# A hybrid layer on one core: four batches stage by stage, or two groups of two batches with stages interleaved

## What is computed

```
x = x + ssm(ln(x))     # gated selective scan, 16 states per channel
x = x + ffn(ln(x))     # dense + 2 of 8 experts, chosen once per batch
x = x + att(ln(x))     # retention, then attention over its output
x = x + ffn(ln(x))     # the same weights as above
```

## Time and profile before

| | us |
|---|---|
| median of 3 runs | 1385.68 (1381.11 to 1390.2) |
| the profiled execution | 1391.36, span 1389.4 |
| busy of the span: PE, ACT, DVE, POOL | 1071.3, 975.3, 742.7, 325.7 |
| granted PE clock, mean | 0.915 of full speed |

### The profile page before, as it was taken

How to read it: one execution, slowest core, us unless ns; L and a number is a source line. 1 busy time by engine, 2 the same in 40 slices (tenths; PEclk the granted TensorE clock), 3 DMA queues, 4 the chain that set the end, 5 groups by cost and what they waited for, 6 DMA issues and landing times. The chain is left out here.

```text
span 1389.4 us, 17492 instructions
## 1 busy us (share of the span) xinstructions
PE 1071.3 (77%) x5850; PEld 393.9 (28%) x5850; DVE 742.7 (53%) x1012; ACT 975.3 (70%) x884; POOL 325.7 (23%) x194
## 2 busy tenths in 40 slices
PE   4748777777799956777446888888888888679996
PEld 3213333333344422332341111111111111134443
DVE  5869998987566648998481001200300300256664
ACT  3767665754688832221336999999999999658885
POOL 3117776766111114665100000000000000011110
PEclk8769999999899978998777999999999999879998
DMA  2000100100100000000001111111111111000002
GB/s 73 0 16 30 31 30 30 60 30 31 32 30 30 31 24 0 0 0 1 8 0 33 24 24 32 37 24 28 22 33 34 24 24 28 11 31 31 30 30 61
DMA packets 24188, 36.48 MB, mean 26 GB/s; under 512 B 7362, under 2 KB 11970, under 8 KB 24130
## 3 DMA queue, kind: packets, MB, share of 16 engines
q1 hardware_dynamic: 24130, 35.71, 9.5%
HBM read 16.82 MB, written 6.29 MB: 17 GB/s over the span
## 5 line engine op out<-in xcount | busy, mean ns | idle before, releaser
L1674 ACT ACTIVATE att_prob<-att_s_ps 128x1536 f32<-128x1536 f32 x342 | 459.2, 1912 | 7.4 <-PE att_s_ps L1588 7.3
L1603 PE MATMUL att_o_ps<-att_prob,att_va 128*32 128x512 f32 x2048 | 273.9, 607 | 0.5 <-ACT att_prob L1674 0.5
L1705 DVE COPY att_o_sb<-att_o_ps 128x512 f32<-128x512 f32 x32 | 22.1, 691 | 381.7 <-PE att_o_ps L1603 381.7
L1588 PE MATMUL att_s_ps<-att_q_st,att_k_st 32*128 32x512 f16 x1024 | 134.4, 388 | 80.8 <-ACT att_prob L1674 76.1
L685 POOL TENSOR_TENSOR scan_hc<-scan_state,scan_c_rep 128x1024 f32<-128x1024 f32 x64 | 151.9, 2392 | 71.9 <-DVE scan_state L642 71.7
L787 POOL TENSOR_TENSOR ffn_veps<-ffn_mv,all_eps 128x4 f32<-128x4 f32 x16 | 9.1, 570 | 575.3 <-DVE ffn_mv L944 575.3
L642 DVE TENSOR_TENSOR_SCAN scan_state<-scan_decay,scan_drive_ps 128x1024 f32<-128x1024 f32 x64 | 142.9, 2270 | 0.3 <-ACT scan_decay L615 0.3
L282 PE MATMUL scan_y_ps<-scan_hc,all_ident 128*128 128x512 f32 x256 | 130.2, 634 | 8.3 <-DVE scan_y_sb L661 6.2
L1588 PEld LDWEIGHTS att_s_ps<-att_q_st,att_k_st 32*128 32x128 f16 x1024 | 33.1, 91 | 327.2 <-ACT att_prob L1674 315.9
L619 ACT ACTIVATE scan_c_rep<-scan_c_ps 128x1024 f32<-128x1024 f32 x64 | 65.4, 1022 | 80.4 <-PE scan_c_ps L282 80.1
L1012 DVE SCALAR_TENSOR_TENSOR ffn_hid_lo<-ffn_hid,ffn_share,ffn_hid_hi 128x1024 f16<-128x1024 f32 x64 | 81.9, 1283 | 48.8 <-ACT ffn_hid_hi L920 48.1
(11 more groups left out here) (215 smaller groups left out, 1505.8 us busy)
## 6 DMA issues: line engine op xcount, KB each, us to landing
ffn_w_sel<-w_split SPq DMA_DIRECT2D x16, 512.0 KB, 3.2
w_split<-scan_w_parts SPq DMA_DIRECT2D x8, 512.0 KB, 2.9
att_q_st<-hv_part SPq DMA_DIRECT2D x64, 64.0 KB, 2.1
att_k_st<-hv_part SPq DMA_DIRECT2D x64, 64.0 KB, 2.1
ln_x_half<-in_x SPq DMA_DIRECT2D x8, 256.0 KB, 2.8
scan_w_raw<-in_w1e SPq DMA_DIRECT2D x8, 256.0 KB, 3.2
scan_w_raw<-in_w2e SPq DMA_DIRECT2D x8, 256.0 KB, 3.4
out<-store_out SPq DMA_DIRECT2D x8, 256.0 KB, 2.4
```

The costliest lines, as they stand in the source:

```text
L1588: last = pe.matmul(s_ps[e % 2][:, n, :], k_st[rows, g % 2, kc * P:(kc + 1) * P], q_st[rows, g % 2, HALVES[half]], start=True, stop=True)
L1603: last = pe.matmul(o_ps[half][32 * j:32 * j + 32, :], va[:, g % 2, kc, j, :], prob[:, (GH * v + j) % RING, :], start=kc == 0, stop=kc == K ...
L1674: act.activation(prob[:, first % RING:first % RING + n, :], s_ps[e % 2][:, 0:n, :], ACT.Exp).then_inc(exped.sem, 1)
```

## The change

Batches 0 and 1 form the first group, 2 and 3 the second. `hybrid_layer` runs load, layer norms and scan inputs for all four, then the selective scan of the first group alone. `group` then runs `mixture`, `queries_and_keys` and `attention` on the first group, with the second group's scans as `following`. The second group's `mixture` holds four feed-forwards (the first ones of batches 2 and 3, the second ones of 0 and 1) and the retentions of 2 and 3; its attention is plain. A last `mixture` holds the second feed-forwards of 2 and 3.

`mixture` replaces `ffn` and `retention`. It is one block in slots s. A feed-forward batch takes 24 slots, 12 for each half of 512 tokens, with the same operations at half the width; y is made by ACT instead of DVE, and x is turned directly, without ACT's staging copy. A retention starts its norm at slot 25 (batch 0 of the list) or 49, and has 16 units of half width (8 rows, two halves of time), in two slots of three from 8 slots after its norm, or one a slot if no feed-forward lies beside. The decay is made as a tanh, halved and shifted by DVE (`open_gate`). Loops are written out. The nine weight splits lie in 32 scan steps, at 1, 4, 7, ... 25. Constants of retention, queries, attention and the scan's `a_neg` are made in `load_constants`. A stage's semaphores are cleared by POOL at its end.

```diff
+                sp.dma_start(w_all[:, 0:len(RET_MATS), :], d["ret_mats"]).then_inc(ret_loaded, 16)
+                sp.dma_start(w_all[:, len(RET_MATS):W, :], d["wsv"]).then_inc(ret_loaded, 16)
+                sp.dma_start(t.head_sum[:, :, :], d["head_sum"]).then_inc(att_loaded, 16)
+                sp.dma_start(t.qk_mats[:, :, :], d["att_mats"]).then_inc(att_loaded, 16)
+                sp.dma_start(t.qk_rows[:, :, :], d["bqk"]).then_inc(att_loaded, 16)
+                sp.dma_start(t.wo[:, :], d["wo"]).then_inc(att_loaded, 16)
...
+                act.wait_ge(ret_loaded, 16 * 2)
+                act.activation(t.ret_hi[:, :, :], w_all[:, :, :], ACT.Copy, scale=WS).then_inc(ret_high, 1)
...
+                for k in range(E + 1):
+                    sp.wait_ge(w_scaled.sem, w_scaled.before(k, 0, 1))
+                    sp.dma_start(w_raw[:, 0, :], t.dram["w1e"][k] if k < E else t.dram["w1m"]).then_inc(w_loaded, 16)
+                    sp.dma_start(w_raw[:, 1, :], t.dram["w2e"][k] if k < E else t.dram["w2m"]).then_inc(w_loaded, 16)
+                    if k:
+                        sp.wait_ge(w_low.sem, w_low.at(k - 1))
+                        sp.dma_start(t.dram["w_split"][k - 1],
                                      w_parts[:, :, :, :].rearrange("p w h f -> p (w h f)")).then_inc(w_stored, 16)
...
-        SPLITS = (3, 11)
+        SPLITS = tuple(1 + 3 * k for k in range(E + 1))
...
+                def enlarge(k):
+                    act.wait_ge(w_loaded, (k + 1) * 32)
+                    act.wait_ge(w_low.sem, w_low.before(k, 0, 1))
                     act.activation(w_large[:, :, :], w_raw[:, :, :], ACT.Copy, scale=WS).then_inc(w_scaled.sem, 1)
...
+                for k in range(N * NS):
+                    b, n = divmod(k, NS)
+                    act.wait_ge(scanned.sem, scanned.before(b, n, 4))
+                    act.activation(decay[:, n % 4, :], t.dt_t[batches[b]][:, :], ACT.Exp,
+                                   scale=t.a_neg[:, n:n + 1]).then_inc(decayed.sem, 1)
+                    act.wait_ge(c_spread.sem, c_spread.at(b, n))
+                    act.wait_ge(weighed.sem, weighed.before(b, n, 4))
+                    act.activation(c_rep[:, n % 4, :], c_ps[:, :], ACT.Copy).then_inc(c_copied.sem, 1)
+                    if k in SPLITS:
+                        enlarge(SPLITS.index(k))
+                    if k - 1 in SPLITS:
+                        m = SPLITS.index(k - 1)
+                        high_part(m, t.dense if m == E else w_parts)

...
+    norm_at = [(FIRST, "ffn", 0)] + [(1 + 8 * i, "ffn", i + 1) for i in range(N - 1)]
+    norm_at += [(RUN + 1 + RUN * r, "ret", r) for r in range(R)]
+    LAST = RUN * N + LAG + 2
+    if R:
+        LAST = max(LAST, norm_at[-1][0] + 10 + 3 * UNITS // 2 + 6)
+    RET_Q = [q for q, (_, kind, _) in enumerate(norm_at) if kind == "ret"]
+
+    def norms(s, offset):
+        return tuple((q, kind, i) for q, (at, kind, i) in enumerate(norm_at) if at + offset == s and at != FIRST)
+
+    def products_at(s):
+        return tuple((r, p) for r in range(R) for p in range(8) if norm_at[RET_Q[r]][0] + 6 + p == s)
+
+    def unit_slot(r, w):
+        return norm_at[RET_Q[r]][0] + 8 + (3 * w // 2 if r + 1 < N else w)
+
+    def units_at(s):
+        return tuple((r, w) for r in range(R) for w in range(UNITS) if unit_slot(r, w) == s)
+
+    def sums_at(s):
...
+                def up(s):
+                    i, half, m, k, c = place(s)
+                    if m == 0:
+                        pe.wait_ge(z_rest.sem, z_rest.at(i, half))
+                    if k and c == 0:
+                        pe.wait_ge(e_loaded[k - 1], 16 * (i + 1))
+                    if s >= 2:
+                        pe.wait_ge(gelued.sem, gelued.at(0, s - 2))
+                    parts(h_ps[s % 2][:, :], weights(k, 0, 0, c), weights(k, 0, 1, c), z_hi[:, i, HALVES[half]],
+                          z_lo[:, i, HALVES[half]], True, True).then_inc(upped.sem, 1)
+
+                def down(s):
+                    i, half, m, k, c = place(s)
+                    if m == 0 and s:
+                        pe.wait_ge(y_made.sem, y_made.at(0, s // M - 1))
+                    pe.wait_ge(rested.sem, rested.at(0, s))
+                    parts(o_ps[:, :], weights(k, 1, 0, c), weights(k, 1, 1, c), hid_hi[:, s % 4, :], hid_lo[:, s % 4, :],
+                          m == 0, m == M - 1).then_inc(downed.sem, 1)
...
+                def key_value(r, w):
+                    h, n = divmod(w, HD)
+                    if r or w >= 2:
+                        pe.wait_ge(scanned.sem, scanned.at(r, w - 2))
+                    m = len(RET_MATS) + n
+                    parts(kv_ps[w % 2][:, :], t.ret_hi[:, m, :], t.ret_lo[:, m, :], z_hi[:, N + r, HALVES[h]],
+                          z_lo[:, N + r, HALVES[h]], True, True).then_inc(v_made.sem, 1)
+
...
+                for s in range(LAST + 1):
+                    if s < RUN * N:
+                        up(s)
+                    if s == 1:
+                        spread_shares(0)
+                    if 0 <= s - LAG < RUN * N:
+                        down(s - LAG)
+                    for q, kind, i in norms(s, 0):
+                        turn_x(q, kind, i, 0)
+                    for q, kind, i in norms(s, 3):
+                        turn_z(q, 0)
+                        turn_x(q, kind, i, 1)
+                    for q, kind, i in norms(s, 6):
+                        turn_z(q, 1)
+                    for q, kind, i in norms(s, 9):
+                        if kind == "ffn":
+                            gate(q, i)
+                    for q, kind, i in norms(s, 13):
+                        if kind == "ffn":
+                            spread_shares(i)
+                    for r, p in products_at(s):
+                        make(r, p)
+                    for r, w in units_at(s):
+                        key_value(r, w)
+                    for r, x in sums_at(s):
+                        add_heads(r, x)
+
+            @block.scalar
+            def _(act):
...
+                def gelu(s):
+                    i, half, m, k, c = place(s)
+                    act.wait_ge(upped.sem, upped.at(0, s))
+                    if s >= 3:
+                        act.wait_ge(rested.sem, rested.at(0, s - 3))
+                    if k == 1 and c == 0 and half == 0:
+                        act.wait_ge(be_loaded[i], 32)
+                        act.wait_ge(gate_steps.sem, gate_steps.at(i, 6))
+                    b1 = t.col("b1m", c) if k == 0 else be[:, i, k - 1, c:c + 1]
+                    act.activation(hid[:, s % 3, :], h_ps[s % 2][:, :], ACT.Gelu_apprx_tanh, bias=b1,
+                                   scale=1.0 / WS).then_inc(gelued.sem, 1)
+                    act.wait_ge(gelued.sem, gelued.at(0, s))
+                    if s >= 4:
+                        act.wait_ge(downed.sem, downed.at(0, s - 4))
...
+                def output(s):
+                    i, half, m, k, c = place(s)
+                    act.wait_ge(downed.sem, downed.at(0, s))
+                    act.wait_ge(biased.sem, biased.at(i, 2))
+                    if s // M:
+                        act.wait_ge(added.sem, added.at(0, s // M - 1))
+                    act.activation(y[:, :], o_ps[:, :], ACT.Identity, bias=bias[:, i, 2:3],
...
+                def rest(s):
+                    i, half, m, k, c = place(s)
+                    dve.wait_ge(casted.sem, casted.at(0, s))
+                    dve.scalar_tensor_tensor(hid_lo[:, s % 4, :], hid[:, s % 3, :], weight_of_expert(i, k),
+                                             hid_hi[:, s % 4, :], ALU.mult, ALU.subtract).then_inc(rested.sem, 1)
+
...
+                def open_gate(r, h):
+                    dve.wait_ge(copied.sem, copied.at(r, 4 * h + 1))
+                    dve.tensor_scalar(g_sb[:, HALVES[h]], g_sb[:, HALVES[h]], 0.5, 0.5, ALU.mult,
+                                      ALU.add).then_inc(opened.sem, 1)
+
+                def outer(r, w):
+                    h, n = divmod(w, HD)
+                    if n == 0:
+                        dve.wait_ge(copied.sem, copied.at(r, 4 * h))
+                    dve.wait_ge(v_made.sem, v_made.at(r, w))
+                    dve.scalar_tensor_tensor(kv_ps[w % 2][:, :], kv_ps[w % 2][:, :], t.bsv_large[:, n:n + 1],
+                                             k_sb[:, HALVES[h]], ALU.add, ALU.mult).then_inc(kv_done.sem, 1)
+
+                def scan(r, w):
+                    h, n = divmod(w, HD)
+                    if n == 0:
+                        dve.wait_ge(opened.sem, opened.at(r, h))
+                    dve.wait_ge(kv_done.sem, kv_done.at(r, w))
+                    if r or w >= HD:
+                        dve.wait_ge(weighed.sem, weighed.at(r, w - HD))
+                    if h:
+                        dve.wait_ge(scanned.sem, scanned.at(r, w - HD))
+                    dve.tensor_tensor_scan(mem[:, n, :], g_sb[:, HALVES[h]], kv_ps[w % 2][:, :],
```

(61 more changed lines are left out.)

1096 lines of the change are left out of this document (429 added, 667 removed).

## The result

The changed kernel takes 1441.68 us (median of 4 runs, 1439.36 to 1447.19), the kernel before 1385.51 beside it: ratio 1.0411, 95% interval 1.0366 to 1.0456. It is 4.1% slower. The forecast was 1382 within 1325 to 1424: wrong, in the sign and in the range. The profiled execution has a span of 1437.2 us (1389.4 before), mean granted clock 0.902. The other 8 us are in no row here.

The account below looks back on a forecast made before the run. No one engine was taken to bound the whole: DVE is busiest in scan and retention, PE in feed-forward, ACT in attention. The terms summed to -3.5 us, from 1385.7 to 1382, range 1325 to 1424.

Parts of the forecast that it names:

- Scans, -106: Selective scan, two batches alone instead of four, 250 us before: 106 us less, bounds -118 and -98.
- each loop 1 us longer: Selective scan: slower bound, -98, with each of the eight weight-split loops 1 us over the 14.0 or 12.6 worked out.
- Feed-forward, +8 and +15: Mixture: eight batches at 36.5 us instead of 35.5, +8, bounds -8 and +38; a third run-up and drain, +15.
- Retention, -12: Mixture: retention takes 153 us instead of 165, partly beside feed-forward, change -12, bounds -50 and +12.
- the round of three slots at 6.8 us: Retention beside feed-forward: three slots with two units take about 6.8 us instead of 4.6; 28 us a batch in all.
- Attention, +88: Attention in two calls, 319 and 253.5 us, against 484.7 in one: +88, bounds +68 and +115.
- Start, +7.5: First block: constants moved there delay the x loads, +7.5 us, bounds +3 and +10.
- Queries and keys: Queries and keys: 2 x 30 us instead of 65, change -5, bounds -9 and +3.
- The half chain is too long: Rival, feed-forward half slots: gelu, cast and low part outlast PE's 2.6 us; +38, 1420 us; chance 0.25.
- main case: Whole kernel: the summed terms hold, 1382 us, between 1362 and 1402; chance 0.42.
- The waits fill: Rival, mixture and first attention: PE, ACT and DVE streams run ahead of each other; -40, 1342 us; chance 0.33.

Follow-up runs that it names:

- Experiment 1: Changed kernel with two buffers for the split weights, so ScalarE's split no longer waits for the previous low part and store: 1408.49 us, ratio 1.0171.
- experiment 5: Changed kernel with both halves of each interleaved block's first normalisation done side by side: 1419.99 us, ratio 1.0248 to the kernel before.
- experiment 2: Changed kernel with the last feed-forward done by the kernel before's code in slots of 1024: 1429.27 us, ratio 1.0311 to the kernel before.
- experiment 3: Changed kernel with feed-forward and retention one after the other, in the kernel before's instructions of 1024: 1413.40 us, ratio 1.0206.
- experiment 7: Changed kernel with POOL's retention product cut to 32 of 512 columns, most of the retention's output left out: 1432.40 us, ratio 1.0347.
- experiment 4: Changed kernel with all four batches' scans in the scan stage, none beside attention, weight splits 7 steps apart: 1466.41 us, ratio 1.0570.

## Why the prediction was wrong, step by step

- **Scans, -106: failed by 14.** The loop was named, with the right members, and its bound (each loop 1 us longer, -98) was too near. The step that failed is the sum of one loop: it followed ACT, DVE and POOL and left out PE, whose queue stands behind the delayed copy of c (1.95 us in the first loop, 8.84 at the batch's end). Eight loops took 116 instead of 106, and the lead to the first low part 13.7 where the sum left 7. Experiment 1 gives 32 of the 141 us back; the granted clock at the batch's end was left out too, and half of that projection's 3.75 us is its price.
- **Feed-forward, +8 and +15: the largest failure.** A half slot at 1.35 was right (1.33). Wrong was that everything else of a batch was carried over at its old price. The run-up was taken as before's 14.6, though the first normalisation's halves now come one after the other: 5.4 more in the last block (experiment 5), in three blocks. The inner normalisations were put at PE's and ACT's own work; one costs some 6 us by counting, there are five. By itself the last block was 94.6 against 88, and experiment 2 shows 8.7 lost against whole slots. The two terms add to +23. With two batches at 94.6 in two of the blocks, and four at 94.6 + 2 x 33 + 2 x 6 = 173 in the other, feed-forward would be 362 against 313.7 before, an estimate of +48.
- **Retention, -12: failed by about 13**, by the same estimate (527.8 - 362 = 166, 165 before, 153 forecast). In the second block the five halves that hold the two retentions take 156.2 us, 74 more than 16.5 each; 56 were forecast, and the end of the last feed-forward normalisation, some 6, is in them. The step that failed is the round of three slots at 6.8 us: in a half with nothing but units beside it is 7.5 (30.0 for 12 slots). DVE is busy 26.7 of these 30 us: it is nearly the bound there. In the second block it is busy 25 us more than in wide instructions (experiment 3), some 16 of them by the meetings with POOL (experiment 7, where the five halves come 7 us shorter without them) and some 9 by halving. The prediction named the meetings and put them at 6 us within its 28 a batch. The tail came as forecast: 16 units in 49.7 us for 50, some at 2.80 with the wait of 0.92 and more of them at 3.5 at the lower clock.
- **Attention, +88: held** (+93), by its parts: 323 for 319, 254.3 for 253.5. That scans can be hidden there is shown by experiment 4.
- **Start, +7.5: too high by 5**; x came 6.2 later, and part of that was made up before the first scan. **Queries and keys: held.**
- **The rivals.** "The half chain is too long" had a time (1420) nearer the measured 1441.7 than the main case and the right occasion, DVE doing a normalisation or a scan first, but not the mechanism: where DVE is free, a half slot shows no such delay. "The waits fill" is refuted: PE waits 51 us for the retention's scans.
- **The range.** It is said to hold the bounds of both big terms; those of scans and attention added to 1382 give 1350 to 1417, so how 1325 and 1424 came about isn't shown. The mixture's upper bounds (+38 for +8, +12 for -12) were in neither end. With these 54 us more the upper end would have been 1471, and the measured time under it.

Shown are the loop and its price, the run-up in the last block, the tail's wait and the meetings. Of the inner normalisation the price rests on counting slots in one trace; its split between queueing and plain work is shown by one experiment, and weakly. The two estimates of +48 and 166 rest on that count. What the granted clock costs was varied by no experiment.

## What to carry to other kernels

When work is halved to interleave it, price every instruction that stays beside the main chain again: run-up, normalisation and fixed parts. A stage whose helpers had two slots' time now has one, and a chain kept in one buffer becomes a loop over all engines, also over the one that only queues behind it. Before interleaving two streams, add up the engine they share at the new widths: here DVE's busy share rose to 89% where both ran, and in the second block running the streams one after the other was as fast. Then look for pairs of instructions that lengthen each other: most of DVE's extra time in the second block (16 of 25 us) came from them.

## What had not been expected of the hardware

A low part of 512 columns that starts beside POOL's product takes 1.65 instead of 0.72 us, while POOL's product keeps its 1.27 (rows in experiment 7). Where the low part is first, it is the product that takes 1.69:

```profile
940.95 0.72 DVE L1127 SCALAR_TENSOR_TENSOR mix_hid_lo<-mix_hid,mix_share,mix_hid_hi 128x512 f16<-128x512 f32 x1
941.11 1.69 POOL L1225 TENSOR_TENSOR mix_qm<-mix_mem,mix_q_sb 128x512 f32<-128x512 f32 x1 [2.48 <-DVE mix_mem L1152]
```

Yet half of that lengthening cost no time (19 us longer, 7 to 9 lost). And two traces of a stretch with nothing changed in it, from the start of the first block to the first exponential, in the changed kernel and in experiment 1, differ by 3.7 us (228.0 and 224.3), at granted clocks of 0.80 and 0.82: differences under 4 us between single traces aren't read here.
